# Weaving the second layer's weight net into the ranking of destinations, from batch 13 on

## The reference

```python
src, dst = (edge_index[0], edge_index[1])
deg_out = segment_sum(edge_weight, src); deg_in = segment_sum(edge_weight, dst)   # layer 0
...
# layer 1, the weight net: 8 attributes of an edge -> 256 weights
h = silu(edge_attr @ fc_w1 * (1.0 / sqrt(8)))
h = silu(h @ fc_w2 * (1.0 / sqrt(64)))
w = h @ fc_w3 * (1.0 / sqrt(64))
wA, wB, wC, wD = split(w, 4, axis=1)
...
m0a = wA * es * sh0
# layers 0, 1, 2, 3: messages gathered by one end of the edge and summed by the other
msg = xt[src] * norm[:, None]
agg = segment_sum(msg, dst, num_segments=n_nodes)
```

## Time and profile before

| | us |
|---|---|
| median of 3 timed runs | 8992.88 (8976.12 to 9014.39) |
| span of the profiled execution | 10600.9 |
| scatters of rec_s, first to last start | 53.2 to 1195.1 |
| scatters of rec_d, first to last start | 1249.7 to 2450.4 |
| first gather behind the preparation | 3173.0 |
| busy over the span: PE, DVE, ACT, POOL | 5863.5, 5886.6, 2842.6, 5780.3 |

### The profile page before, as it was taken

One profiled execution on the slowest core, in us unless ns is written; L12 is line 12 of the kernel. 1 busy time (PEld: TensorE's weight loads), 2 busy tenths in 40 slices (PEclk: granted clock), 3 DMA queues, 4 the chain that ended last, 5 costly groups with the idle time before them and its releaser, 6 DMA issues. The chain is left out here.

```text
span 10600.9 us, 101980 instructions
## 1 busy us (share of the span) xinstructions
PE 5863.5 (55%) x21277; PEld 3328.7 (31%) x21277; DVE 5886.6 (56%) x17788; ACT 2842.6 (27%) x9329; POOL 5780.3 (55%) x6087
## 2 busy tenths in 40 slices
PE   2211344447864444555557777765555578855554
PEld 1100233334433333333334121233333333333332
DVE  8942533330016666544445999976556579942223
ACT  0000000005862222100003787752222236600000
POOL 5776566661006667566662888834555520046665
PEclk9999855558986777777777999987666679966666
DMA  2000111113553333433332555535666645523333
GB/s 79 6 6 6 32 47 46 44 35 125 177 193 100 95 94 95 110 93 93 93 84 76 172 173 171 173 78 153 183 185 186 186 127 175 157 78 93 93 93 83
DMA packets 782889, 1136.27 MB, mean 107 GB/s; under 512 B 161213, under 2 KB 631923, under 8 KB 775629
## 3 DMA queue, kind: packets, MB, share of 16 engines
q0 software_dynamic: 246400, 552.44, 19.7%
q1 hardware_dynamic: 535885, 577.31, 16.7%
HBM read 872.21 MB, written 257.00 MB: 107 GB/s over the span
## 5 line engine op out<-in xcount | busy, mean ns | idle before, releaser
L1159 POOL DMA_INDIRECT ring<-scaled_table,idx_s x832 | 790.0, 949 | 1159.0 <-DVEq L192 771.8
L1028 POOL DMA_INDIRECT big<-x_table,rec_d_sb x808 | 807.1, 999 | 1070.7 <-DMA x_table<-big 721.6
L1759 POOL DMA_INDIRECT ring<-att_table,rec_d_sb x808 | 774.8, 959 | 759.1 <-DVE acc L1869 319.9
L1438 PE MATMUL bank<-ring,wts 128*128 128x512 f32 x1664 | 944.0, 653 | 377.6 <-DVE acc L1425 157.2
L1360 POOL DMA_INDIRECT ring<-y_table,idx_s x832 | 814.9, 979 | 404.1 <-DVEq L192 181.5
L333 POOL DMA_INDIRECT rec_s<-acc,big x784 | 842.3, 1074 | 350.4 <-issue 254.7
L333 POOL DMA_INDIRECT rec_d<-x_res,big x784 | 753.1, 961 | 502.2 <-DVE big L596 254.2
L1159 POOL DMA_INDIRECT ring<-h_table,rec_d_sb x808 | 766.2, 948 | 443.0 <-issue 230.8
L2112 PE MATMUL bank<-ring,acc 128*128 128x256 f32 x1664 | 712.4, 578 | 487.6 <-issue 310.8
L1120 PE MATMUL bank<-big,acc 128*128 128x256 f32 x1616 | 573.6, 527 | 627.6 <-issue 367.9
L1193 PE MATMUL bank<-ring,acc 128*128 128x256 f32 x1616 | 590.8, 511 | 572.7 <-DVE acc L1181 337.2
(11 more groups left out here) (346 smaller groups left out, 12798.6 us busy)
## 6 DMA issues: line engine op xcount, KB each, us to landing
weights_dram<-acc SPq DMA_DIRECT2D x104, 1024.0 KB, 4.5
ring<-weights_dram SPq DMA_DIRECT2D x832, 128.0 KB
rows_spill<-ring SPq DMA_DIRECT2D x808, 128.0 KB
big<-rows_spill SPq DMA_DIRECT2D x808, 128.0 KB, 2.2
ring<-key_dram SPq DMA_DIRECT2D x49, 1024.0 KB
big<-dl_dram SPq DMA_DIRECT2D x50, 512.0 KB
ring<-y_table,idx_s POOLq DMA_INDIRECT x832
ring<-scaled_table,idx_s POOLq DMA_INDIRECT x832
```

The costliest lines, as they stand in the source:

```text
L1028: g.indirect_dma_start(out=xg[:, c % RG, :], out_offset=None, in_=x_table, in_offset=bass.IndirectOffsetOnAxis(ap=recd3i[:, c, D_IDX:D_IDX ...
L1159: g.indirect_dma_start(out=slot[:, c % ring_len, :], out_offset=None, in_=table, in_offset=bass.IndirectOffsetOnAxis(ap=index(c), axis=0)) ...
L1438: pe.matmul(ps[6 + u % 2], oh1[c // 4 % 2][:, c % 4, :], mid[:, c % 2, 0:512], start=(c % GS == 0), stop=(c % GS == GS - 1)).then_inc(summ ...
L1759: g.indirect_dma_start(out=ag[:, n % R3, :], out_offset=None, in_=att_table, in_offset=bass.IndirectOffsetOnAxis(ap=recd3i[:, n, D_IDX:D_I ...
```

## The change

The net's steps are cut into pieces of 23 and written into the ranking's loop from b = FIRST = 12 on (37 batches), on PE, ACT and SP. DVE's part of the net (clear, wait for the weights, scale them) goes between `rank_vector(12)` and `rows_vector(10)`, and so do its waits. The ranking gets one bank of PSUM for prefixes (before two) and one for picks (before two), the rows of batch b - 2 are made in step b, and PE's picks of b - 1 wait until DVE has used those of b - 2. The third matmuls go round two banks (before three), and the net's other three results share one. The number tables and the degrees' turn and store follow after the net. The count of DMAs, of matmuls and of everything else stays as it was.

```diff
-        key_bank, pick_bank = [ps[1], ps[6]], [ps[4], ps[6]]
+        key_bank, pick_bank = [ps[1], ps[6]], ps[4]
+        NG = NCS // 8
+        FIRST = 12
+        STEPS = up(8 * NG + 14, NBATCH - FIRST) // (NBATCH - FIRST)
+        third_bank = [ps[0][:, 0:D], ps[6][:, 0:D]]
+        hidden_bank, turn_bank = ps[3], ps[3][:, 0:P]
+        def mlp_steps(b):
+            return range(max(0, (b - FIRST) * STEPS), max(0, min(8 * NG + 14, (b - FIRST + 1) * STEPS)))
...
-            for b in range(NBATCH):
-                if b >= 2:
-                    sp.wait_ge(bcast_used.s, bcast_used.n(b - 1))
...
+            for b in range(-1, NBATCH + 1):
+                if b + 1 < NBATCH:
+                    if b >= 1:
+                        sp.wait_ge(bcast_used.s, bcast_used.n(b))
...
+                if b == FIRST:
+                    fc_sync()
+                for n in range(3, NG + 3):
+                    if 8 * n - 2 in mlp_steps(b):
+                        mlp_sync(n)
...
                 ins.then_inc(lanes_hot.s, 1)
+                for n in mlp_steps(b):
+                    mlp_scalar(n)
...
-            pe.wait_ge(rows_ready.s, NBATCH + max(0, b - 1))
+            pe.wait_ge(rows_ready.s, NBATCH + b)
...
-            ins.then_inc(step_done.s, 1)
+                if b >= NBATCH - 1:
+                    ins.then_inc(step_done.s, 1)
+                if b == FIRST:
+                    pe.wait_ge(fc_scaled.s, 1)
+                for n in mlp_steps(b):
+                    mlp_tensor(n)
...
-            v.wait_ge(step_done.s, step_done.n(min(b + 3, NBATCH + 1)))
+            v.wait_ge(step_done.s, step_done.n(b + 3))
...
-            for b in range(NBATCH + 3):
+            for b in range(NBATCH + 2):
                 if b < NBATCH:
                     rank_vector(b)
-                if b >= 3:
-                    rows_vector(b - 3)
+                if b == FIRST:
+                    mlp_vector()
+                if b >= 2:
+                    rows_vector(b - 2)
...
-                    if c >= 3:
-                        pe.wait_ge(w_kept.s, c - 2)
-                    pe.matmul(ps[5 + c % 3][:, 0:D], h2[half, i % 2, (k // 2) * P:(k // 2) * P + P],
+                if c >= 2:
+                    pe.wait_ge(w_kept.s, c - 1)
+                pe.matmul(third_bank[c % 2], h2[half, i % 2, (k // 2) * P:(k // 2) * P + P],
```

191 lines of the change are left out of this document (94 added, 97 removed).

## The result

The changed kernel takes 9525.4 us (median of 4 runs, 9516.24 to 9533.59) where the kernel before takes 8984.5 us (4 runs): a ratio of 1.0607, 95% interval 1.0587 to 1.0626, 541 us slower. The forecast was 9100 us with 9280 as its upper end. The direction was right, the size was not.

The account below looks back on a forecast made before the run. POOL's rec_d scatters end the preparation before (T + 988); after, PE's serial woven batches do: T + 24 + 1047 (37 x 28.3) + 27 = T + 1098. That is 110 us slower: 8993 + 110 = 9103, said 9100 us, range 8960 to 9280.

Parts of the forecast that it names:

- T: End of POOL's scatters of rec_s in the preparation, forecast at 1156 us and alike for both kernels.
- cover of 131 us: In the kernel before, the net was to end some 131 us ahead of the last rec_d scatters, which hide it.
- wait for rec_s: In step 12 of DVE's loop, DVE stands from about 964 us until 1156 us: 190 us.
- wait for rows: In each woven batch, PE's picks wait for DVE's rows of batch b - 2: 2.9 us.
- the group: Net's group of eight chunks on PE with two banks: 6.4 us, 2.86 groups a woven batch, 17.3 us after savings.
- the picks: PE's picks in each woven batch, up to the next ranking: 3.8 us with the hop.
- the clock: PE leaves busy picks at the lower clock level; 1.0 us a batch added for net steps run so.
- lower clock throughout: Rival: PE stays at the lower clock, group 10.1 us, woven batch 46 us, time about 9750 us; chance 0.05.
- This wait alone costs nothing, because POOL covers it: DVE's 190 us stop at batch 12 costs nothing, since POOL has 202 us of scatters ready meanwhile.
- moved DMAs: SP's key loads behind a batch's last net load, some 16 us for 1 MB, keep their lead; priced at nothing.
- The 136 us I could not place: Rebuilding the timed run from the profile removed 1744 us where 1608 were wanted; the 136 us overshoot stayed in the range.
- the stalls would be real: By the fixed 6 us profile-time rule, profile gaps exist in timed runs and the net is on the path; chance 0.12.

Follow-up runs that it names:

- f0_before_sbuf: The control: kernel before, with the ranking's row of numbers and triangle read from SBUF instead of PSUM bank 5; 9078.4 us, ratio 1.0107, chip without gaps.
- e5_two_thirds: Kernel before, not woven, with two PSUM banks for the third product instead of three; 10956.41 us, ratio 1.0363, chip with gaps.
- f1_three: Changed kernel with three banks for the third product, row of numbers and triangle read from SBUF; 9302.18 us, ratio 1.0347 to before, without gaps.
- f3_three_first25: Changed kernel with three banks and SBUF reads, the net starting at the 26th batch (FIRST 25); 9116.61 us, ratio 1.0152 to before, without gaps.
- e1_first25: Changed kernel, still two banks, with FIRST 25 in place of 12; 10976.54 us, ratio 1.0305 to the kernel before, chip with gaps.
- h0_two_fill1: Kernel before with two banks for the third product and one extra unread matmul ahead of each chunk's wait; 9705.24 us, ratio 1.0782, without gaps.
- g0_two_fill: Kernel before with two banks for the third product and four extra unread matmuls ahead of each chunk's wait; 10942.19 us, ratio 1.0318, with gaps.
- g2_three_ahead_first25: Changed kernel with three banks, SBUF reads, four net steps ahead of the picks, start at 26th batch; 10478.77 us, ratio 0.9881 to before, with gaps.
- h1_all_three_again: Changed kernel with three banks, SBUF reads, four net steps ahead, start at 26th batch, run again; 9106.53 us, ratio 1.0122 to before, without gaps.

## Why the prediction was wrong, and where it was right

**Right: the frame.** Which resource ends the preparation was read correctly from a profile that shows the opposite. T was 1160 us (1156 forecast). The cover of 131 us in the kernel before is seen in the control (128 us, with both ends some 30 us late). The wait for rec_s took 187 us (190). The wait for rows was 3.2 us a batch (2.9), ranking 4.0 (3.5). An unwoven ranking batch of the control takes 10.0 us, as allowed. The weave is paid for in full, because TensorE works in order and the scatters had been hiding the net.

**Wrong: the group.** The step that failed is "With two banks a third matmul waits for the copies of the last but one; I follow the group's rows and find about 0.5 us in each of its two runs of chunks ... I take 6.4 us". That the stops take the place of the wait for records was right: TensorE waits 0.5 us for records in the whole woven stretch. The step has two faults. The stops are longer than I found: a full-clock group is 7.4 us, 1.0 us over my 6.4. Two stops of 0.6 us show as such, and a third of 0.5 us hides in a row of four parts: line 796 at 2695.04 us in `e5_two_thirds` takes 1.18 us, where the same four parts take 0.70 at 2605.63 us in the kernel before. And I priced the group at the upper level, while with two banks the clock falls: 10.06 us a group with two banks and nothing else changed, 9.7 us in the woven batches. The term was 17.3 us and measured 27.7; 385 of 481 us.

The banks are not all of it. With the third bank back the net steps are 20.8 us, 3.5 over the forecast, at a clock of 0.78 in the woven stretch of `f1_three` (1300 to 2400 us). 1.4 us a batch of this is waiting for records; the rest is the lower clock, by argument and not by a run.

**Wrong: the picks**, 3.8 us forecast, 6.4 measured, 96 us. I took them from a batch at the upper level; in the woven kernel most run at the lower one. The stop for the rows ahead of them has a part in it, but does not explain it: dummies in the stop took them to 5.0 and net steps ahead with three banks to 5.1, yet the same steps ahead with two banks left them at 6.2, with no stop ahead.

**Too small: the clock.** I had one sighting of the lower level, 1.77 us for 0.99, and put 1.0 us on it. The row was right. The rival "lower clock throughout" priced a group at that level with 10.1 us; the traces give 9.57 with three banks and 11.85 with two. Its chance of 0.05 rested on the net's clock of 0.96. That row belongs to three banks; the change takes one away, so it was no evidence about the net after. The truth lies between forecast and that rival: 41.3 us a batch against 28.3 and 46.

**Half wrong: "This wait alone costs nothing, because POOL covers it".** The scatters did run on through it. But 13 more batches ahead of the net are worth 186 us once the banks are repaired (`f3_three_first25`), since ranking batches fit into the wait that are later on the path: 13 x 13.3 = 173 us of ranking, wait for rows and picks. With two banks no run tested this, as `e1_first25` had no such wait.

**Small: moved DMAs.** In the changed kernel TensorE waits 0.5 us for records. They do become late when the net is quick: 45 us in `f1_three` over the woven stretch. An unwoven ranking batch on the changed kernel takes 13.5 us where I allowed 10; the wait for rows, present there too (2.8 us), and slower picks (5.9 us) make the difference, and the wait for rec_s covers it.

**The 136 us I could not place** are in the traces without gaps, all but about 10 of them. The last scatter is some 27 us later than I had it (2172 against 2145 us). The first gather follows it by 55 us and not by 28 (2323.5 - 2268.3 in `f0_before_sbuf`). The four gather stages take 1057.1, 1031.2, 1010.6 and 1041.2 us there, 74 us over my floors. Together this is some 128 us.

What makes the gaps on some chips is open. That they go with the chip was seen on four chips; I compared a profile from one sort with times from the other. The passage that named a fixed difference between profile and time, some 6 us (the Trainium skill, Runtime: NRT & Kernel Launch, the preamble/postamble breakdown), was dismissed for the wrong reason. On one chip, span and time of an execution differ by 2 us (10692.8 and 10694.65), the time being the longer. So no run here shows the 6 us, but "the stalls would be real" holds on a chip with gaps.

## What to carry to other kernels

Before taking a PSUM bank from a pipeline, price the group at both levels of TensorE's clock (7.4 and 11.9 us here), and put real weight on the lower one; the clock of the stretch as it was (0.96) says nothing about it. When work moves into an engine's program order beside other work, and its buffers shrink to make room, test the shrunken buffers alone first: one such run found most of this loss, and four that moved waits or the start about found little. Compare a profile only with times from the same chip, and an edit only with its like on the same sort of chip: on a chip with gaps the net ends last, so that neither the later start nor slower scatters can show in the time there.

## What the runs showed of the hardware

- Two output banks in place of three took TensorE's granted clock in the net from 0.96 to 0.68, though it stood idle for a smaller share of the time (132.0 us of 1050 in place of 105.2 of 690). A group with two banks takes 7.38 us wholly at the upper level and 11.85 at the lower; with three, 6.30 and 9.57.
- TensorE at full busy time in the profile can stay at half its clock: 850.00 us busy of 850.00 at 0.50 with one extra matmul a chunk (`h0_two_fill1`, without gaps), and 0.98 with four (`g0_two_fill`, with gaps), which was 5 us a group faster.
- A VectorE comparison with both inputs in SBUF stretched an indirect DMA's issue on POOL from 0.96 to 2.98 us; the same operation with one input in PSUM did not (0.97 us at most among the 784 scatters of rec_d in the changed kernel), and sixteen short ones in its place stretched it to 1.17 us on the timeline shown.
- Chips differ by 18% on this kernel (8982 and 10593 us), through gaps that stand where POOL issues indirect DMAs. The same change was a gain on one sort (0.988, `g2_three_ahead_first25`) and a loss on the other (1.012, `h1_all_three_again`).
